# A fused state-space and mixture-of-experts kernel: PSUM banks given out anew, softplus sums moved to GpSimd, carries copied by ScalarE, and a new order of work

## The reference, cut to what matters

```
# layer 1: selective scan, inner width 256, 16 states per channel
xi, res = x @ in_proj_w.T;  xi = silu(causal_conv4(xi));  dt, B, C = xi @ x_proj_w.T
delta = softplus(dt @ dt_proj_w.T + b)
h_t = exp(delta*A) * h_{t-1} + delta*B*xi ;  y = sum_n(h*C) + xi*D ;  y*silu(res) @ out_proj_w.T
# layer 2: FP8-quantised 128x128 linear layer
# layer 3: scan with 16 states and one step size: delta = mean(softplus(x @ W.T + b))
h_t = exp(delta*A) * h_{t-1} + delta*(x @ B.T) ;  y = h @ C.T + D*x
# layer 4: RMS norm, router softmax over 8 experts, top 2, capacity 512 in token order;
# an expert is (gelu(h@Wg) * (h@Wu)) @ Wd; tokens over capacity take a small side net instead
```

## Time and profile before

| | |
|---|---|
| runs (three) | 481.4, 481.6, 482.89 us; median 481.6 |
| profiled execution | 480.05 us, its span 478.3 us |
| busy share of the span | PE 85%, DVE 85%, ACT 67%, POOL 48% |
| granted TensorE clock, mean | 0.934 of full speed |
| instructions | 6017 |

### The profile page before, as it was taken

The page is one execution under the profiler, slowest core; times in us unless marked ns, Lnnn a source line. Parts: engine busy times, 40 slices in busy tenths (PEclk is TensorE's granted clock), DMA queues, the critical chain, the costliest instruction groups (busy, mean ns, idle before and its releaser), DMA issues.

```text
span 478.3 us, 6017 instructions
## 1 busy us (share of the span) xinstructions
PE 407.7 (85%) x1680; PEld 246.4 (52%) x1680; DVE 408.9 (85%) x890; ACT 319.4 (67%) x521; POOL 230.5 (48%) x203
## 2 busy tenths in 40 slices
PE   4989777679268999999967799999496999999993
PEld 3333222243124777755423478766132687778873
DVE  4569999999999999999999889999989765675654
ACT  3887246458544999999963778874746579587231
POOL 0049599899574475456964724656962000000000
PEclk9989989999597999999997599999789899999997
DMA  8496398998245455556853723575750000000000
GB/s 288 168 332 223 110 302 292 320 311 277 86 176 187 166 175 177 181 161 194 275 185 105 248 88 120 165 229 158 251 200 2 0 1 0 3 0 23 1 1 22
DMA packets 22065, 74.19 MB, mean 155 GB/s; under 512 B 2320, under 2 KB 4368, under 8 KB 21648
## 3 DMA queue, kind: packets, MB, share of 16 engines
q1 hardware_dynamic: 22032, 73.82, 46.7%
HBM read 72.50 MB, written 1.31 MB: 154 GB/s over the span
## 4 chain that ended last, share of the span: by engine, by line
PE 50%; DVE 26%; issue 11%; ACT 7%; POOL 4%; DMA 2%; SPq 1%; DVEq 0%; ACTq 0%; POOLq 0%
PE ps_g L719 11%; PE ps_y L626 10%; PE ps_u L764 10%; DVE ps_state L1127 7%; PE ps_u L719 6%; DVE product L1144 4%; PE ps_state L719 2%; DMA hidden<-w_up 2%; DVE drive L1127 2%; POOL drive L999 2%; DVE delta L1111 2%; DVE delta L1113 2%; PE ps_y L764 1%; POOL product L1020 1%; DVE stats L1154 1%
## 5 line engine op out<-in xcount | busy, mean ns | idle before, releaser
L999 POOL TENSOR_TENSOR drive<-du,b_row 128x512 f32<-128x512 f32 x128 | 164.9, 1308 | 51.0 <-DVE ps_state L1127 37.3
L626 PE MATMUL ps_y<-product,par 128*128 128x512 f32 x256 | 135.6, 648 | 21.1 <-DVE product L1144 12.7
L865 ACT ACTIVATE ps_state<-delta,decay_rate 128x512 f32<-128x512 f32 x128 | 85.5, 688 | 58.3 <-DVE product L1144 45.2
L626 PEld LDWEIGHTS ps_y<-product,par 128*128 128x128 f32 x256 | 47.9, 204 | 81.8 <-issue 32.7
L782 ACT ACT_TABLE_LOAD x69 | 88.5, 1283 | 1.9 <-PEq L1385 0.7
L1020 POOL TENSOR_TENSOR product<-drive,c_row 128x512 f32<-128x512 f32 x38 | 48.4, 1274 | 55.3 <-DVE drive L1127 51.3
L1144 DVE TENSOR_TENSOR product<-ps_state,c_row 128x512 f32<-128x512 f32 x90 | 60.2, 679 | 1.3 <-PE ps_y L626 1.0
L764 PEld LDWEIGHTS ps_u<-wd,hidden 128*128 128x128 f32 x448 | 53.8, 192 | 4.9 <-issue 2.0
L1127 DVE TENSOR_TENSOR_SCAN ps_state<-ps_state,carry,drive 128x512 f32<-128x512 f32 x44 | 55.3, 1274 | 0.3 <-ACT ps_state L865 0.3
L1127 DVE TENSOR_TENSOR_SCAN ps_state<-ps_state,drive 128x512 f32<-128x512 f32 x46 | 54.6, 1213 | 0.9 <-ACT ps_state L865 0.8
L764 PE MATMUL ps_u<-wd,hidden 128*128 128x128 f32 x448 | 54.9, 276 | 0.0
(11 more groups left out here) (253 smaller groups left out, 600.5 us busy)
## 6 DMA issues: line engine op xcount, KB each, us to landing
b_row<-bc_dram SPq DMA_DIRECT2D x64, 512.0 KB, 5.0
c_row<-bc_dram SPq DMA_DIRECT2D x64, 512.0 KB, 4.1
x_in<-x_t SPq DMA_DIRECT2D x4, 256.0 KB, 6.9
gelu<-w_gate SPq DMA_DIRECT2D x1, 1024.0 KB, 9.1
hidden<-w_up SPq DMA_DIRECT2D x1, 1024.0 KB, 10.9
wd<-w_down SPq DMA_DIRECT2D x1, 1024.0 KB, 12.8
out<-acc SPq DMA_DIRECT2D x4, 256.0 KB, 2.4
par<-params SPq DMA_DIRECT2D x1, 598.0 KB, 6.6
```

The costliest lines, as they stand in the source:

```text
L626: mm(ps_y[:, :], ident, product[:, g % PRODUCTS, :], start=False, stop=(n == STATE - 1)).then_inc(y_pe, 1)
L865: nc.scalar.activation(ps_state[g % RING][:, :], delta[:, c % 2, h, :], ACT.Exp, scale=decay_rate[:, h, n:n + 1]).then_inc(decay_act, 1)
L999: nc.gpsimd.tensor_tensor(drive[:, g % DRIVES, :], du[:, h, :], b_row[:, m % ROWS, n % 2, :], ALU.mult).then_inc(drive_pool, 1)
```

## The change

**PSUM.** The eight banks become `ps_y`, three `ps_state`, `ps_tail` (all stages of all tails), `ps_net0` and `ps_net1` (gate and up), and `ps_acc` (down). `tail_bank` is gone. A tail now waits for the counts of the tail before (`late`) and no longer for the nets before it. The stages of a tail wait for one another's reads of `ps_tail`: the Bx matmul is issued after relu, the mean after ACT's copy of Bx, the first half of r3 after decay and drive. The last chunk's nets go round five banks.

**Softplus.** ACT makes 1+exp (Identity, bias 1) as well. DVE makes (1+e)-1-e in one operation; POOL (`settle`) makes relu minus that and adds ln. In chunk 0 (layer 1) and in the last chunk (layer 3) these two stay on DVE. That is 12 adds for layer 1 and 6 for layer 3 on POOL, and 12 Identities on ACT.

**Carries.** ACT copies them, just before it overwrites the state bank. **Rings.** PRODUCTS is 7 in place of 8, GROUP (gelu tiles) 2 in place of 3. **Router input.** x3 is normalised first and hn is x3 times rms, so DVE's scale3 and shift3 (L1222, L1223) go. Gate waits for the two parts of hn in place of the logits.

```diff
-PRODUCTS = 8
+PRODUCTS = 7
-GROUP = 3
+GROUP = 2
...
-        ps_g = [bank("ps_g0"), bank("ps_g1")]
-        ps_u = [bank("ps_u0"), bank("ps_u1")]
-        ps_acc = ps_u[1]
+        ps_tail = bank("ps_tail")
+        ps_net = [bank("ps_net0"), bank("ps_net1")]
+        ps_acc = bank("ps_acc")
...
         def banks_of(c):
-            return [*net_banks, *ps_state] if c == LAST else net_banks
+            return [*ps_net, *ps_state] if c == LAST else ps_net
...
 # tensor, tail k == 0
-                    if c == LAST:
-                        pe.wait_ge(product_dve, count(by_vector, STEPS - 1))
-                        pe.wait_ge(state_dve, STEPS)
-                    elif c:
-                        pe.wait_ge(hidden_dve, 2 * NETS * c)
-                        pe.wait_ge(gelu_act, 2 * NETS * c)
-                        pe.wait_ge(acc_dve, NETS * c)
+                    if c:
+                        after(pe, tail_dve, c - 1, "late")
...
 # tensor, gate i == 0
-                    after(pe, tail_dve, c, "lg")
-                    after(pe, tail_act, c, "x3")
+                    after(pe, tail_act, c, "hi")
+                    after(pe, tail_dve, c, "lo")
+                    if c + 2 < CHUNKS:
+                        after(pe, pre_act, c + 2, "relu1")
...
 # scalar, pre k >= 7
+                    do(pre_act, delta[:, q, h, :], sp_exp[:, :], ACT.Identity, bias=1.0)
                     do(pre_act, sp_ln[:, h, :], sp_exp[:, :], ACT.Ln, bias=1.0)
...
 # scalar, step
                     else:
+                        if old // UNITS % PER_BATCH == 0:
+                            was = old % UNITS
+                            made(act, old)
+                            nc.scalar.copy(carry[:, was // STATE, was % STATE:was % STATE + 1],
+                                           ps_state[old % RING][:, CHUNK - 1:CHUNK]).then_inc(carry_act, 1)
+                            carried(act, old)
                         made(act, old)
...
 # gpsimd
+            def settle(c, h):
+                q = c % 2
+                if c == 0:
+                    return
+                after(pool, rest_dve, c, f"rest{h}")
+                after(pool, pre_act, c, f"relu{h}")
+                nc.gpsimd.tensor_tensor(delta[:, q, h, :], sp_relu[:, h, :], delta[:, q, h, :],
+                                        ALU.subtract).then_inc(delta_pool.sem, 1)
+                after(pool, delta_pool, c - 1, f"b{h}")
+                after(pool, pre_act, c, f"ln{h}")
+                nc.gpsimd.tensor_tensor(delta[:, q, h, :], delta[:, q, h, :], sp_ln[:, h, :],
+                                        ALU.add).then_inc(delta_pool.sem, 1)
...
 # vector, make_delta
-                do(pre_dve, v.tensor_scalar(delta[:, q, h, :], sp_exp[:, :], 1.0, -1.0, ALU.add, ALU.add))
-                own(pre_dve, c, f"t{h}")
-                do(pre_dve, v.tensor_tensor(delta[:, q, h, :], sp_exp[:, :], delta[:, q, h, :], ALU.subtract))
-                own(pre_dve, c, f"a{h}")
-                do(pre_dve, v.tensor_tensor(delta[:, q, h, :], delta[:, q, h, :], sp_relu[:, h, :], ALU.add))
-                own(pre_dve, c, f"b{h}")
+                do(rest_dve, v.scalar_tensor_tensor(delta[:, q, h, :], delta[:, q, h, :], 1.0, sp_exp[:, :],
+                                                    ALU.subtract, ALU.subtract))
+                if c:
+                    return
...
 # vector, finish
-                if c % PER_BATCH == 0:
-                    v.tensor_copy(carry[:, h, n:n + 1], state[:, CHUNK - 1:CHUNK]).then_inc(carry_dve, 1)
```

More of the change, by code:

```diff
@@ L280, in build @@
         product = sb("product", [P, PRODUCTS, CHUNK])
-        def l1_of(c, name):
-            name = {"ln": "abs", "t": "sp"}.get(name, name)
-            i = L1_NAMES.split().index(name)
-            if c == CHUNKS - 1:
-                place = product[:, i, :]
-            elif i < 6:
-                place = gelu[:, i // 2, i % 2, :]
-            else:
-                place = hidden[:, 1, 0, :]
-            return place[0:STATE, :] if name in ("step", "decay", "drive") else place
         carry = sb("carry", [P, HALVES, STATE])
@@ L310, in build @@
         rms_inv = sb("rms_inv", [P, BLOCKS])
-        scale3 = sb("scale3", [P, BLOCKS])
-        shift3 = sb("shift3", [P, BLOCKS])
         x3 = sb("x3", [P, BLOCKS, P])
+        l1_abs, l1_relu, l1_exp = (x.rearrange("p j d -> p (j d)") for x in (x1_bias[:, :, :], x1[:, :, :], x3[:, :, :]))
+        l1_ln = l1_abs
+        l1_sp = sb("l1_sp", [P, CHUNK])
+        l1_drive = sb("l1_drive", [STATE, CHUNK])
+        l1_decay = sb("l1_decay", [STATE, CHUNK])
         hn_t = sb("hn_t", [P, CHUNK])
@@ L414, in build @@
         tail_pe = Marks(sem("tail_pe"), "r1 x1t ffn x2t dlt bx mean r3 hnt logits counts")
-        tail_act = Marks(sem("tail_act"), "l1 rstd1 x1 x1q ffn l2 rstd2 x2 x2t abs exp relu ln step decay "
-                         "l3 rstd3 l4 rms hn hnt hi x3 exps acc")
-        tail_dve = Marks(sem("tail_dve"), "st1 mo1 sh1 r2 st2 mo2 sh2 t a b sp drive scan keep st3 mo3 vr msq sh3 inv s3 "
-                         "f3 lo lg top cen tot tinv probs sort where wf p1 p2 picked late over kept w0 w wsum xw red psum pbef")
+        tail_act = Marks(sem("tail_act"), "l1 rstd1 x1 x1q ffn l2 rstd2 x2 x2t abs relu exp one ln bx decay "
+                         "l3 rstd3 x3 l4 rms hn hnt hi exps acc")
+        tail_dve = Marks(sem("tail_dve"), "st1 mo1 sh1 r2 st2 mo2 sh2 rest drive scan keep st3 mo3 sh3 vr msq inv "
+                         "lo lg top cen tot tinv probs sort where wf p1 p2 picked late over kept w0 w wsum xw red psum pbef")
         tail_pool = Marks(sem("tail_pool"), "bias")
+        l1_pool = Marks(sem("l1_pool"), "b sp")
+        l1_dve = Marks(sem("l1_dve"), "b sp")
         gate_pe = sem("gate_pe")
@@ L430, in after, with delta_made, l1_made @@
             eng.wait_ge(marks.sem, marks.done(c, name))
+        def delta_made(eng, c, h):
+            if c == 0:
+                after(eng, first_dve, 0, f"delta{h}")
+            else:
+                after(eng, delta_pool, c - 1, f"delta{h}")
+        def l1_made(eng, c):
+            if c == LAST:
+                after(eng, l1_dve, 0, "sp")
+            else:
+                after(eng, l1_pool, c, "sp")
         def tokens(c):
@@ L650, in tail @@
                     for j in range(BLOCKS):
-                        last = turn(block_of(tail_bank(c, "x1t")[:, :], j), x1[:, j, :], ident)
+                        last = turn(block_of(ps_tail[:, :], j), x1[:, j, :], ident)
                     last.then_inc(tail_pe.sem, 1)
@@ L662, in tail @@
                     for j in range(BLOCKS):
-                        last = turn(block_of(tail_bank(c, "x2t")[:, :], j), x2[:, j, :], ident)
+                        last = turn(block_of(ps_tail[:, :], j), x2[:, j, :], ident)
                     last.then_inc(tail_pe.sem, 1)
@@ L755, in down @@
                 if e == 0:
-                    after(pe, tail_dve, c, "late")
-                    if c == LAST:
+                    if c:
                         pe.wait_ge(acc_dve, NETS * c)
@@ L835, in pre @@
                     if h:
-                        after(act, pre_dve, c, "a0")
+                        after(act, rest_dve, c, "rest0")
                         after(act, pre_act, c, "ln0")
@@ L853, in step @@
                 if n == 0:
-                    after(act, pre_dve, c, f"delta{h}")
+                    delta_made(act, c, h)
                 if g == 0:
@@ L922, in tail @@
                     rsqrt(tail_act, c, var_log[:, :], "l3", moments[:, :, 1], eps[:, 0:1], rstd[:, :])
-                if k == 10:
+                if k == 11:
+                    after(act, tail_dve, c, "sh3")
+                    normalise(tail_act, x3, lambda j: block_of(ps_tail[:, :], j), rstd, shift)
                     use(EXP_LN)
@@ L926, in tail @@
                     rsqrt(tail_act, c, var_log[:, :], "l4", mean_sq[:, :], eps[:, 1:2], rms[:, :])
-                if k == 11:
-                    after(act, tail_dve, c, "f3")
-                    normalise(tail_act, hn, lambda j: block_of(tail_bank(c, "r3")[:, :], j), scale3, shift3)
                 if k == 12:
+                    after(act, tail_act, c, "rms")
+                    for j in range(BLOCKS):
+                        last = nc.scalar.mul(hn[:, j, :], x3[:, j, :], rms[:, j:j + 1])
+                    last.then_inc(tail_act.sem, 1)
+                if k == 13:
                     after(act, tail_pe, c, "hnt")
@@ L977, in _ @@
             nc.gpsimd.memset(eps[:, 1:2], RMS_EPS).then_inc(pool_const, 1)
+            def settle(c, h):
+                q = c % 2
+                if c == 0:
+                    return
[7 more added lines that the diff above has]
+                                        ALU.add).then_inc(delta_pool.sem, 1)
             def make_du(c, h):
-                after(pool, pre_dve, c, f"delta{h}")
+                delta_made(pool, c, h)
                 if c:
@@ L1007, in tail @@
```

(29 more changed lines are left out.)

145 lines of the change are left out of this document (70 added, 75 removed), and 188 rows, old and new, of the table PLACES.

## The result

The changed kernel takes 465.72 us (median of 4 runs, 463.45 to 468.1), the kernel before 481.5 beside it (4 runs, 479.4 to 482.89): a ratio of 0.9676, 95% interval 0.9615 to 0.9738. A repeat in another set of runs gave 465.4 against 476.4, 0.9759 (0.970 to 0.9819). Single executions that ran over 1.5% above the fastest of their kernel are left out of every ratio and median here. So the gain is 11 to 16 us. I had forecast 475, some 7 us faster: right in sign, and between four and six tenths of the size. The profiled execution took 465.05, its span is 463.2.

A forecast was written before the change was run, and what follows sets the result against it. DVE was taken to bound up to chunk 0's nets, PE those nets and the end. Stages of 159.4 + 57.2 + 46.0 + 54.1 + 42.8 + 112.0 gave 471.5 against 478.3, so 475 us; range 457 to 492, the forecast's own 466 to 480.

The forecast's parts named there:

- stage 6: From the end of the last scan to the end of the span: PE-bound, 112.0 us against 104.9 before.
- surcharge: Added after the last scan: 4.3 us for waits on two net banks and 2.8 for late gate/up groups.
- the four groups: Four PE gate/up groups of three matmuls, 0.70 us each, ahead of the last finish before, now following it: 2.8 us.
- Stage 5: From the last join of chunk 1 to the end of the last scan: 42.8 us against 53.5.
- Stage 2: From the first to the last join of chunk 0: 57.2 us against 43.9, set by DVE.
- DVE is the longer: In the nets of chunk 0: DVE has 57.2 us, PE 49.1 before 4.3 for two banks.
- Stage 3: From the last join of chunk 0 to the first of chunk 1: PE-bound, 46.0 us against 71.8.
- Stage 1: From the start to the first join of chunk 0: 159.4 us against 162.4, with DVE relieved of 17.7.
- my sign of being right: In the changed profile: DVE busy some 30 us less in all (409 to about 379), POOL some 23 more.
- A: Rival: DVE's relief counts in full, last scan ends before 345 us, median 458; chance 0.14.
- B: Rival: POOL takes DVE's place, above 90% before a first join no earlier; median 482, no change; chance 0.15.
- C: Rival: two net banks decide, PE waits above 20 us, chunk 0's joins span above 66; 491 us, slower; chance 0.29.

The follow-up runs named there:

- old_sums_late: Kernel before, order and banks kept, layer 1's softplus adds of chunks 1 to 3 on POOL, each pair right ahead of its du: 480.24 us, 1.0048.
- old_sums_pool: Kernel before, order and banks kept, layer 1's softplus adds of chunks 1 to 3 on POOL among the chunk before's steps: 483.8 us, 1.0104.
- sums_on_dve: Changed kernel with all 18 softplus adds moved from POOL back to DVE: 481.23 us, 1.0101 to the kernel before.
- chunk0_multiply4: Changed kernel with POOL multiplying 4 units of chunk 0 by C in place of 8, DVE the other 4: 466.18 us, 0.9725 to the kernel before.

## Why the prediction was wrong, step by step

The predicted span is 8.3 us too long (471.5 against 463.2). By stages: -1.4, +4.3, -2.0, -0.6, -3.7, -4.9. The time itself, 465.72, lies inside my range of 457 to 492 and just under the forecast's own, 466 to 480.

**The step that failed is stage 6, "Stage 6 is 112.0"**: its base of 104.9 and both terms of the surcharge of 7.1 us on it. The stage measured 107.1, so the surcharge was 2.2. The miss has two parts. The first is the base. In the kernel before, that stage held two stretches at half the clock, one around the last scan and one behind a gap of PE (1.49 busy of 2 us from 426):

```profile
372.00:374.00 2.00, 2.00 (x4) 0.74 (x3) 1.90 (x6) 1.51 (x2) 0.00 (x0) 0.50 0.00 0
...
428.00:430.00 2.00, 2.00 (x8) 1.60 (x8) 1.79 (x10) 1.97 (x3) 0.00 (x0) 0.75 0.00 0
430.00:432.00 2.00, 2.00 (x6) 1.57 (x5) 1.86 (x18) 1.27 (x3) 0.00 (x0) 0.50 0.00 0
432.00:434.00 2.00, 2.00 (x14) 1.42 (x13) 0.79 (x7) 1.37 (x3) 0.00 (x0) 0.90 0.00 0
```

In the changed kernel and in its repeat the granted clock of stage 6 is 1.00 until the last five us, when PE has finished; the end is low in every run. The old order with neither drop is old_sums_late, 101.7 us (same gap of PE, full clock). So 3.2 of the 4.9 us are in the base that I took over from one execution. old_sums_pool, with the second drop alone, has 103.2: 1.5 for that one, and the other 1.7 of the kernel before go with the first, which put four sums of PE at 3.52 us for 1.96.

The second part is the surcharge itself: at like clock it is 107.1 - 101.7 = 5.4, 1.7 under my 7.1. Of it the banks are 1.8, not 4.3. A wait costs what I said and more (5.6 over 9, 0.62 us), but five banks have waits too, and PE's own work fills part of the rest: what counts is the difference of the stages. The remaining 3.6 go with a later start of chunk 2's nets. That is near my 2.8, but by luck, for my reason was wrong: I had the four groups ahead of the last scan before and behind it after. In the kernel before all 192 gate and up matmuls of the experts of chunks 2 and 3 already start behind the last scan, in old_sums_late three of them ahead of it. What is new is that PE makes tail 2's logits, for which it waits on DVE, and two more matmuls of sums between the last scan and the first gate matmul. In the changed kernel, whose last scan ends at 356.08:

```profile
356.81 1.03 PE L688 MATMUL ps_tail<-par,hn_t 128*128 128x8 f32 x8 [0.78 <-DVE hn_part L1255]
357.69 1.96 PE L626 MATMUL ps_y<-product,par 128*128 128x512 f32 x4
359.09 1.97 PE L718 MATMUL ps_net<-hn_part,wg 128*128 128x512 f32 x6
```

and in old_sums_late, whose last scan ends at 375.38:

```profile
374.35 1.26 PE L732 MATMUL ps_u<-hn_part,wg 128*128 128x512 f32 x3
```

The first gate matmul comes 3.0 us behind the scan in the one and 1.0 ahead of it in the other. No run takes this start back alone, so the 3.6 are a remainder and not a measured price.

**Stage 5, 3.7 us too long.** 1.9 is my count: DVE's list behind the last join of chunk 1 held one accumulate and one product fewer than I gave it. The rest is idle time: 0.8 us in the changed kernel (39.1 less 38.32), 2.5 in the old stage (53.5 less 50.96) that I had carried along. It is a mis-sized term too, and a fault of bookkeeping.

**Stage 2, 4.3 too short.** I had DVE at 57.2 and PE well under it, at 49.1 and 4.3 for the banks. Both are full: PE 60.64 of 61.5 us, DVE 59.75, and lines of PE make up over 70% of the chain of waits there. So the step "DVE is the longer" failed for PE's side. I gave PE six more identity sums, 5.2 us; line L626 takes 19.75 us there in 43 records for 9.07 in 18 before, some 12 units more, and tail 1's 32 matmuls of x_in, res_gate, x and x_q came in, which I had at nothing. On DVE one accumulate (1.3 us), L1209 at 1.72 us for 0.84 and the router's small operations make up the difference. Stage 3 was 2.0 shorter than predicted.

**Stage 1: right, a little timid.** POOL 118.61 us busy against 118.8 predicted; DVE 119.24, 10.4 less than before, where I had 17.7 off and 1.7 on. I chose 3 us from a range of -8 to +1; it was -4.4. The experiments fit both ends failing: more on either engine lengthens the stage, less on both did not shorten it.

**The size of the relief.** DVE's busy time fell by 21.8 us, not by the 30.5 that my sign of being right named. My sum added the lengths of records; busy time counts an overlap once. Added up as I did, DVE's records fell from 463.2 to 434.5 us, 28.6 less, so that sum was nearly right. The gap to 21.8 is mostly the carries, whose 6.8 us lie over their neighbours. As relief they are 2.3 us at most, 1.2 of them in stage 1 where I had 3.5, and worth nothing in time in either order (two runs).

The fused operation of layer 1 came at a mean of 1.09 us, near my 1.17. In sums_on_dve, with the 18 adds off POOL, it is 0.91. The Trainium skill (SBUF — State Buffer, Who interferes with whom) gives the direction and says that the loser waits for the whole instruction. The trace agrees, and shows in the last section a loser that stood while four went by. The small operations, which I had left out, grew: L1263 (192 to 625 ns on average) and L1193 (329 to 652). For L1193 most of that came with the new order and not with the adds: without them it is 588.

**The rivals.** A is wrong: last scan at 356.1, not before 345. B's condition on POOL came true (93%), its result not: the join came earlier. C is wrong: stage 2 is 61.5 us, under 66, and PE's waits 13.9 us, under 20. What no rival held is what the experiments show: of the sums and the order, neither paid without the other.

## What to carry to other kernels

Before work is moved off a busy engine, ask what its list waits for next: 9.8 us less on DVE in stage 1 gave 0.6 us there in the old order, and the moved sums gave the whole 11 to 16 in one that had other work to put there. A stage's length from one execution contains its own clock drops; look at the granted clock slice by slice before it is taken as a base. Take the price of a small operation from the starts of its neighbours, not from its record. Before a mean is used, look at the longest one behind it.

## What was not expected of the hardware

A tiny operation of VectorE can stand for several GpSimd instructions in a row. L1193's mean of 652 ns is one instruction of 4.65 us among twelve with a median of 162 ns. POOL runs drives back to back over it, the rest of one and three whole ones. The 128x4 operation ends at 106.90, 0.02 us behind the last of them:

```profile
100.72 6.16 POOL L1026 TENSOR_TENSOR drive<-du,b_row 128x512 f32<-128x512 f32 x5
...
102.25 4.65 DVE L1193 SCALAR_TENSOR_TENSOR shift<-moments,rstd 128x4 f32<-128x4 f32 x1
```

It is there in nine of the ten profiles of the new order, 4.56 to 4.68 us long, each time under four drives; sums_on_dve has it too, so the moved adds are not its cause. In chunk0_multiply4 the longest is 0.91 us, in the kernel before 1.25. Likewise L1263 takes 192 ns twice and 1.05 and 1.07 us twice, both times beside a product of POOL.

Copying one column from PSUM has records of 147 ns on VectorE and 154 on ScalarE, and cost VectorE 0.05 us.

The same gap of PE at 426 us was followed by half the clock in the kernel before and not in old_sums_late; what makes the difference stays open.
